# Value heads quantised in the buffer of the queries and keys, and output rows quantised by GpSimd, in the first attention layer of a two-layer decoder

## The reference, cut to what matters

```python
def act_quant(x):
    scale = 127.0 / jnp.clip(jnp.max(jnp.abs(x), axis=-1, keepdims=True), EPS)
    q = jnp.clip(jnp.round(x * scale), -128.0, 127.0) / scale
    return x + jax.lax.stop_gradient(q - x)
...
xq = act_quant(x)
q = act_quant(heads(bit_linear(xq, Wq)))
k = act_quant(heads(bit_linear(xq, Wk)))
v = act_quant(heads(bit_linear(xq, Wv)))
scores = jnp.einsum('bhtd,bhsd->bhts', q, k) * (1.0 / math.sqrt(D))
w = act_quant(jax.nn.softmax(scores, axis=-1))
y = act_quant(jnp.einsum('bhts,bhsd->bhtd', w, v))
y = y.transpose(0, 2, 1, 3).reshape(B, T, C)
y = act_quant(bit_linear(y, Wp))
...
x = x + _L0_attn_ref(_layernorm(x, axis=-1), L0_attn_Wq, ...)
```

## Time and profile before

| What | Value |
|---|---|
| Time, median of 3 runs | 1777.76 us (1777.14 to 1778.35) |
| The profiled execution's own time | 1782.12 us |
| Its span, from first to last instruction | 1780.3 us |
| Busy over the span | PE 80%, DVE 75%, ACT 57%, POOL 20% |
| The loop of the changed layer | from about 38 to 288 us |

### The profile page before, as it was taken

The page is one execution under the profiler, slowest core; times in us unless marked ns, Lnnn a source line. Parts: engine busy times, 40 slices in busy tenths (PEclk is TensorE's granted clock), DMA queues, the critical chain, the costliest instruction groups (busy, mean ns, idle before and its releaser), DMA issues. The chain is left out here.

```text
span 1780.3 us, 38229 instructions
## 1 busy us (share of the span) xinstructions
PE 1423.0 (80%) x13101; PEld 909.2 (51%) x13116; DVE 1342.5 (75%) x2547; ACT 1009.8 (57%) x1731; POOL 349.8 (20%) x509
## 2 busy tenths in 40 slices
PE   1777785899999999999997645973888699845992
PEld 0455553444444444444446545962666467634891
DVE  6888876688888888888886773548898556585774
ACT  1777763476766766666762432543677355454461
POOL 1122214100000000000000244652333200046241
PEclk9565655999999999999998767986999699958996
DMA  6950001133333333333320243533000000034335
GB/s 135 311 177 1 1 1 35 39 71 73 87 74 90 75 88 78 84 81 78 87 36 2 75 144 113 172 134 97 2 1 0 1 2 0 1 118 128 102 105 163
DMA packets 156618, 136.21 MB, mean 77 GB/s; under 512 B 73729, under 2 KB 137801, under 8 KB 156387
## 3 DMA queue, kind: packets, MB, share of 16 engines
q1 hardware_dynamic: 146627, 111.46, 24.7%
q0 software_dynamic: 7776, 21.28, 3.3%
q10 hardware_dynamic: 2112, 2.10, 0.4%
HBM read 66.85 MB, written 40.30 MB: 60 GB/s over the span
## 5 line engine op out<-in xcount | busy, mean ns | idle before, releaser
L2698 ACT ACTIVATE lat_Pb<-banks 125x896 f32<-125x896 f32 x384 | 328.4, 925 | 148.3 <-PE banks L2594 145.8
L2808 DVE TENSOR_TENSOR lat_dsum<-lat_dsum,lat_Pb 125x896 f32<-125x896 f32 x320 | 349.5, 1092 | 70.1 <-ACT lat_Pb L2698 62.5
L2572 PE MATMUL banks<-lat_Pb,lat_kv 125*64 125x448 f32 x1536 | 309.6, 545 | 0.0
L2594 PE MATMUL banks<-lat_Q,lat_kT 64*125 64x448 f16 x2304 | 256.8, 358 | 3.9 <-DVE lat_QT L2740 1.3
L2594 PEld LDWEIGHTS banks<-lat_Q,lat_kT 64*125 64x125 f16 x2304 | 141.1, 132 | 148.1 <-issue 66.2
L2572 PEld LDWEIGHTS banks<-lat_Pb,lat_kv 125*64 125x64 f32 x1536 | 101.7, 136 | 165.8 <-issue 157.9
L3103 POOL MEMSET moe_one<- 128x16 f32 (+1 forms) x2 | 0.2, 109 | 648.6 <-POOLq L259 648.6
L3152 POOL DMA_INDIRECT sent_outputs<-moe_yb,moe_yidx x98 | 95.7, 976 | 117.3 <-ACT moe_yb L3411 102.1
L3290 PE MATMUL banks<-moe_w2d,moe_gT 88*128 (+3 forms) x780 | 102.5, 282 | 17.6 <-DVE moe_gT L3629 13.6
L3617 DVE COPY moe_xTb<-banks 128x1024 f16<-128x1024 f16 x49 | 33.9, 691 | 80.3 <-PE banks L3257 80.3
L3290 PEld LDWEIGHTS banks<-moe_w2d,moe_gT 88*128 88x128 f16 (+1 forms) x780 | 77.0, 101 | 30.9 <-issue 19.2
(11 more groups left out here) (453 smaller groups left out, 3013.4 us busy)
## 6 DMA issues: line engine op xcount, KB each, us to landing
lat_Q<-lat_QT SPq DMA_DIRECT2D x128, 112.0 KB, 3.5
moe_xb<-sent_rows SPq DMA_DIRECT2D x49, 257.0 KB, 2.9
lat_raw<-in_ctx_dram SPq DMA_DIRECT2D x32, 375.0 KB
sent_rows<-zero SPq DMA_DIRECT2D x1, 7453.0 KB, 40.6
lat_rD<-lat_reciprocals SPq DMA_DIRECT2D x62, 112.0 KB, 2.8
moe_arena<-sent_outputs SPq DMA_DIRECT2D x12, 512.0 KB, 6.7
sent_rows<-zero SPq DMA_DIRECT2D x1, 5140.0 KB, 58.1
sent_outputs<-zero SPq DMA_DIRECT2D x1, 4096.0 KB, 42.0
```

The costliest lines, as they stand in the source:

```text
L2572: ins = nc.tensor.matmul(ps[u * DC:(u + 1) * DC, 6, 0:8 * T], kv[:, par, tt, :], Pb[:, tile_slot(tt, par), u, :], start=tt == 0, stop=tt = ...
L2594: ins = nc.tensor.matmul(ps[0:KP, n % 3 * 2 + q, 0:8 * T], kT[rows, par, 2 * pair + low, 0:KP], Q2[rows, par, w, 8 * u:8 * u + 8, :].rearr ...
L2698: nc.scalar.activation(Pb[:, slot:slot + 2, u, :], ps[0:KP, n % 3 * 2:n % 3 * 2 + 2, 0:8 * T], ACT.Exp, scale=1.0 / QSCALE).then_inc(exp_d ...
L2808: ins = nc.vector.tensor_tensor(dsum[:, par], dsum[:, par], Pb[:, tile_slot(tt, par)], ALU.add)
```

## The change

The buffers `qk` and `vf` become two slices of one buffer `qkv` of 48 heads. One multiplication fills it, ScalarE's L1578 adds MAGIC to all of it, and VectorE subtracts MAGIC and scales the value heads in an instruction of its own behind that of the queries and keys. TensorE's wait before the next projection is on `qq_made` instead of `vf_made`. VectorE's part of the output ends with its scale and factor; GpSimd shifts and scales the output in two instructions ahead of its addition. VectorE's wait on `x_added` moves up to before L1893, and ScalarE's `zc` copy waits for GpSimd's first instruction. The diff, with lines that only declare semaphores left out:

```diff
-        qk = sb("qk", [P, 32, HD])
-        vf = sb("vf", [P, H, HD])
+        qkv = sb("qkv", [P, 48, HD])
+        qk, vf = qkv[:, 0:32, :], qkv[:, 32:48, :]
...
                     if bit and live(i - 2):

                         pool.wait_ge(yo_made, i - 1)
+                        pool.sem_inc(yo_begun, 1)
+                        nc.gpsimd.tensor_scalar(yo[:], zc[:], ax[:, 2:3], MAGIC, ALU.mult,
+                                                ALU.add).then_inc(yo_shifted, 1)
+                        pool.wait_ge(yo_shifted, i - 1)
+                        pool.sem_inc(yo_begun, 1)
+                        nc.gpsimd.tensor_scalar(yo[:], yo[:], MAGIC, ax[:, 1:2], ALU.subtract,
+                                                ALU.mult).then_inc(yo_scaled, 1)
+                        pool.wait_ge(yo_scaled, i - 1)
                         xi = x[:, ds(i - 2, 1), :].rearrange("p o d -> p (o d)")
                         nc.gpsimd.tensor_tensor(xi, xi, yo[:], ALU.add).then_inc(x_added, 1)
...
                         act.wait_ge(qq_made, i + 2)
-                        nc.scalar.activation(qk[:], qk[:], ACT.Identity,
+                        nc.scalar.activation(qkv[:], qkv[:], ACT.Identity,
                                              bias=magic[:, 0:1]).then_inc(qr_made, 1)
...
                         if live(i - 2):
-                            act.wait_ge(yo_made, i - 1)
+                            act.wait_ge(yo_shifted, i - 1)
                         nc.scalar.activation(zc[:], Z, ACT.Copy).then_inc(z_used, 1)
...
-                            pe.wait_ge(vf_made if bit else v_made, i + 2)
+                            pe.wait_ge(qq_made if bit else v_made, i + 2)
...
                         then(nc.vector.tensor_tensor(ax[:, 0:1], ax[:, 0:1], sw[:, 3:4], ALU.mult))
+                        if not isinstance(i, int) or i >= 1:
+                            dve.wait_ge(x_added, i)
                         then(nc.vector.tensor_scalar(ax[:, 1:2], ax[:, 0:1], QEPS, 1.0 / 127, ALU.max,
                                                      ALU.mult))
                         then(nc.vector.reciprocal(ax[:, 2:3], ax[:, 1:2]))
                         then(nc.vector.tensor_tensor(ax[:, 2:3], ax[:, 2:3], sw[:, 3:4], ALU.mult))
-                        if not isinstance(i, int) or i >= 1:
-                            dve.wait_ge(x_added, i)
-                        then(nc.vector.tensor_scalar(yo[:], zc[:], ax[:, 2:3], MAGIC, ALU.mult,
-                                                     ALU.add))
-                        nc.vector.tensor_scalar(yo[:], yo[:], MAGIC, ax[:, 1:2], ALU.subtract,
-                                                ALU.mult).then_inc(yo_made, 1)
+                        s.settle()
+                        dve.sem_inc(yo_made, 1)
...
-                        nc.vector.tensor_tensor(qk[:], pj[:, 0:32, :], fq[:, 0:32].unsqueeze(2)
-                                                .broadcast_to([P, 32, HD]), ALU.mult
+                        nc.vector.tensor_tensor(qkv[:], pj, fq[:].unsqueeze(2)
+                                                .broadcast_to([P, 48, HD]), ALU.mult
                                                 ).then_inc(qq_made, 1)
-                        nc.vector.tensor_tensor(vf[:], pj[:, 32:48, :], fq[:, 32:48].unsqueeze(2)
-                                                .broadcast_to([P, 16, HD]), ALU.mult).then_inc(vq_made, 1)
-                        dve.wait_ge(vq_made, i + 1)
-                        then(nc.vector.tensor_scalar(vf[:], vf[:], MAGIC, MAGIC, ALU.add, ALU.subtract))
-                        nc.vector.tensor_tensor(vf[:], vf[:], dq[:, 32:48].unsqueeze(2)
-                                                .broadcast_to([P, 16, HD]), ALU.mult).then_inc(vf_made, 1)
...
                     nc.vector.scalar_tensor_tensor(
                         qk[:], qk[:], -MAGIC, dq[:, 0:32].unsqueeze(2).broadcast_to([P, 32, HD]),
                         ALU.add, ALU.mult).then_inc(qk_made, 1)
+                    nc.vector.scalar_tensor_tensor(
+                        vf[:], vf[:], -MAGIC, dq[:, 32:48].unsqueeze(2).broadcast_to([P, 16, HD]),
+                        ALU.add, ALU.mult).then_inc(vf_made, 1)
...
-STEPS = {"bit": 25, "rot": 11, "causal": 2}
+STEPS = {"bit": 23, "rot": 11, "causal": 2}
```

More of the change, by code:

```diff
@@ L1305, in self_attention @@
             E2, magic = sb("E2", [P, H, T]), sb("magic", [P, 2])
-            wsum_done, asum_made, vq_made = sem("weight_sums_done"), sem("asum_made"), sem("vq_made")
+            wsum_done, asum_made = sem("weight_sums_done"), sem("asum_made")
             own_weights = sem("dve_weights")
@@ L1311, in self_attention @@
                 sem("heads_multiplied"), sem("heads_shifted"), sem("rows_centered"))
-            yo_made, x_added, e2_made = sem("outputs_made"), sem("outputs_added"), sem("scaled_exp_made")
+            yo_made, x_added, e2_made = (
+                sem("output_scales_made"), sem("outputs_added"), sem("scaled_exp_made"))
+            yo_shifted, yo_scaled, yo_begun = (
+                sem("outputs_shifted"), sem("outputs_scaled"), sem("outputs_begun"))
         elif rot:
```

## The result

| | Before | After |
|---|---|---|
| Time, median | 1778.05 us (6 runs, 1777.14 to 1780.23) | 1787.96 us (6 runs, 1782.65 to 1789.86) |
| Ratio | 1 | 1.0051, 95% interval 1.0041 to 1.0062 |
| Profiled span | 1780.3 us | 1786.1 us |
| Next stage opens (first DMA of `lat_cosK`) | 288.04 us | 296.44 us |

By the ratio the kernel became slower by 9.1 us (7.3 to 11.0); the two medians lie 9.9 apart. The prediction was 5.1 us slower; the time lies inside its range. New are L1962 (value scaling), L1530 and L1534 (GpSimd); its addition is L1538.

The account below looks back on a forecast made before the run. The prediction took a TensorE-ScalarE ring without slack as the bound, not busiest VectorE. Its terms, 2.6 + 0.6 + 0.5 + 0.8 + 0.6 = +5.1 us on 1777.8, gave 1782.9 us, range 1778.5 to 1789.

Parts of the forecast that it names:

- The ring: TensorE and ScalarE hand each other work without slack; L1578 with 768 columns adds 0.20 us in 13 turns, +2.6 us.
- Nothing for VectorE's saving: In the loop, VectorE saves about 1.2 us a turn, credited with nothing because it then waits longer for L1578.
- VectorE sets the pace: Rival: VectorE bounds the loop, so 1.2 us comes off each of 14 turns, -17 us, 1761 us; chance 0.07.
- L2053 before L1828: Busier GpSimd delays VectorE's L2053, which then holds up L1828 in three of 13 turns, +0.6 us.
- The turn at 250.55: L2053 already holds L1828 up there, so the 0.54 us by which VectorE is later lands whole, +0.5 us.
- The end: After the last turn nothing hides GpSimd's shift and scale, 0.6 us each, before the next stage opens, +0.8 us.
- The first turns: The value split starts 1.2 us later, a faster first split gives 0.3 back; +0.6 us at the loop's start.
- The granted clock: TensorE's varying clock, which sets how long L1740 to L2297's end takes; no term in the sum, only a rival.
- the rival: The clock pays it back: 0.2 us less a turn between L1740 and L2297's end, 2.6 us, 1780.3 us; chance 0.14.
- The prediction's own sign of a clock at work: The forecast is wrong if the loop's mean clock moves from 0.61 by more than 0.03.
- The prediction's spread of the products: L1740 to L2297's end, head transposes and weight products, took 2.2 to 3.8 us a turn by the granted clock.
- the prediction's second rival: GpSimd holds VectorE's L2045, L2048 and L2053 0.3 to 0.5 us each, delaying L1828: 5.7 us, 1788 us; chance 0.19.

Follow-up runs that it names:

- the second profile of before: The kernel before, unchanged, profiled once more; its next stage opened at 288.2 us, against 288.0 in its first profile.
- the three fastest kernels: Changed kernel with VectorE shifting all heads instead of ScalarE: 0.9967; also with outputs as before the change: 0.9965; or with GpSimd adding -MAGIC instead of subtracting: 0.9961.
- the slowest: The kernel before with ScalarE's shift over 1536 columns instead of 512, 1024 of them zeros nobody reads: ratio 1.0108.

## Why the prediction was right, and where its size was off

- **The ring: right.** L1578 with 768 columns takes 935 ns (0.93 us by the rows' slope), and L1578 to L1740 grew by 0.21 us a turn; L2307 to the next L1578 stayed at 9.07. The runs with only a longer shift show that it costs time by itself.
- **Nothing for VectorE's saving: right.** It waits 27.2 us for ScalarE instead of 8.3. That VectorE sets the pace fell with it; the half microsecond in the second profile of before is all that any trace shows for it.
- **L2053 before L1828 (+0.6): did not happen.** L2059 ended 6.84 to 7.10 us after L1589's start in the 12 turns, near the 7.2 given, and was never the last: slack of 0.1 us at least. The slower products kept L1828 later.
- **The turn at 250.55 (+0.5): right at its place, gone at the end.** L1839 started 6.72 us behind the shift instead of 6.12. By the last `zc` copy nothing of it was left.
- **The end (+0.8): 1.3.** The row of the new instruction is 0.47 us for the shift and 1.14 for the scale, for the 0.6 each of the prediction. The last turn of the changed kernel, timeline, answers to the earlier trace rows:

```profile
292.87 0.16 DVE L1909 TENSOR_TENSOR bit_ax<-bit_ax,bit_sw 128x1 f32<-128x1 f32 x1
...
293.32 0.47 POOL L1530 TENSOR_SCALAR bit_yo<-bit_zc,bit_ax 128x256 f32<-128x256 f32 x1 [7.43 <-DVEq L1911]
294.00 1.14 POOL L1534 TENSOR_SCALAR bit_yo<-bit_yo,bit_ax 128x256 f32<-128x256 f32 x1 [0.21 <-POOL bit_yo L1530]
295.23 0.72 POOL L1538 TENSOR_TENSOR x_res<-x_res,bit_yo 128x256 f32<-128x256 f32 x1
296.44 0.30 SPq L2345 DMA_DIRECT2D lat_cosK<-in_lat_cos_dram  x1
```

- **The first turns (+0.6): 0.8.** L2029's counterpart moved by 0.90, as the 1.2 less 0.3 of the prediction.
- **The granted clock: the term that was off.** The sum had nothing for it, and the rival had it paying 2.6 us back. It cost 3.6 us between the first two profiles and 5.0 between the means of two each. That is most of the distance from 5.1 to 9.1. The prediction's own sign of a clock at work, a mean of the loop that moves by more than 0.03, did not show it: 0.61 went to 0.60. The prediction's spread of the products, 2.2 to 3.8 us a turn, was read rightly, but taken as even odds around zero; no row of a single kernel could say which way.

So direction and ring were right by the mechanism. The sum without the clock, 5.1 against 4.8 in the profiles, came out so near because errors cancel: the 1.1 us for L2053 and for the turn at 250.55 did not come, and the end, the first turns and the rest of the 12 turns cost 0.9 more than their terms. And that the time lies inside the range is in part luck: its upper end was made of a dearer L1578 and of GpSimd holding VectorE up, and neither came so: L1578 grew by 0.21 us, near the 0.20 taken, and GpSimd never made L2059 the last.

What the runs show of the clock: over the five lengths of the shift, products of 27.7 to 29.9 us with no shift on the ring, 31.4 to 35.0 with the old one, 33.4 to 37.7 with 0.2 us more, 37.6 and 39.1 with 0.4 and 0.8 more; 35.5 with 0.24 more behind the products. Over 12 turns the groups part better: 31.6 to 33.0, 35.2 to 37.2, 37.3 to 40.7, then 40.7 and 43.0, and 38.5. Longer turns go with slower products. By the times, a length added to the ring cost between 1.2 times (768 columns alone) and 2.5 times (1024 columns) what was reckoned for it. That the products' length goes with the granted clock on them is shown by the windows (3.84 us at 0.50, 2.41 at 0.87); why a longer turn goes with less of it there was not settled, and each point rests on one profiled execution or two. The mean clock of the stretch from 75 to 240 us is no answer: 0.63 and 0.59 in the two profiles of before, 0.60 and 0.60 after, 0.60, 0.59 and 0.60 in the three fastest kernels, and 0.64 in the slowest; over all 14 profiles it is 0.56 to 0.64. So what differs is the clock on the products, not its mean. That 1024 columns cost 15 us and 1536 only 19 needs no cause of its own: the two intervals overlap.

## What to carry to other kernels

In a loop of several engines, look for the ring first: the stretches between two instructions that repeat to the hundredth from turn to turn. Work off that ring costs next to nothing as long as it stays off, so an engine's busy share, even the highest, doesn't say what relieving it brings; here VectorE's room was better used to take ScalarE's step over, 5.9 us faster, until VectorE itself was on the path in a third to half of the turns. Where the clock varies within the turn, an added length on the ring can cost more than itself (here 1.2 to 2.5 times), so give the clock a term in the sum, and profile the same kernel twice before reading differences of a few microseconds.

## What the runs showed of the hardware that was not expected

- GpSimd's tensor_scalar on 128x256 float32 took 0.47 us as a multiplication and an addition, 1.14 us as a subtraction and a multiplication, and 0.48 with the subtraction written as the addition of the negative constant.
- VectorE's instructions with two SBUF inputs were not held for the whole of a long GpSimd instruction, seen on one line, L2051, in 12 turns. Timelines of VectorE and GpSimd, changed kernel:

```profile
170.59 0.40 DVE L2051 TENSOR_TENSOR bit_dy<-bit_dy,bit_cy 128x16 f32<-128x16 f32 x1
...
171.52 0.17 DVE L2054 TENSOR_TENSOR bit_fy<-bit_fy,bit_cy 128x16 f32<-128x16 f32 x1
...
172.19 0.53 DVE L2058 TENSOR_SCALAR bit_yq<-bit_yq 128x256 f32<-128x256 f32 x1
172.75 0.43 DVE L2059 TENSOR_TENSOR bit_yq<-bit_yq,bit_dy 128x256 f32<-128x256 f32 x1
```

```profile
170.49 1.14 POOL L1534 TENSOR_SCALAR bit_yo<-bit_yo,bit_ax 128x256 f32<-128x256 f32 x1 [0.21 <-POOL bit_yo L1530]
171.84 0.72 POOL L1538 TENSOR_TENSOR x_res<-x_res,bit_yo 128x256 f32 x1 [0.21 <-POOL bit_yo L1534]
172.77 0.88 POOL L1458 TENSOR_TENSOR bit_xtmp<-x_res,bit_stats_mean 128x256 f32 x1 [0.20 <-POOL x_res L1538]
```

L2051 was issued 0.1 us into L1534, took 0.40 us instead of 0.17, and ended 0.64 us before it; in every other turn it was issued 0.32 us into L1534 and took 0.17 or 0.18. L2054 started 0.11 us before L1534's end and took its normal 0.17. SBUF — State Buffer of the Trainium skill, section Who interferes with whom, calls the ports that the two engines share an exclusive lock, and says that a VectorE instruction with two SBUF inputs contends with a GpSimd instruction that reads SBUF. The collision is there, in both directions: L1458, issued 0.02 us behind L2059, took 0.88 for its usual 0.61. An exclusion for the whole time of L1534 is not what this trace shows. What the prediction's second rival was built on, a delay of L2045, L2048 and L2053 each, came to 0.23 us for L2045's counterpart in every other turn and to nothing for the other two; L2058, beside the addition L1538, took 0.53 for its usual 0.29.
